# One table of numbers: the last quarter of the units in another order and in other PSUM banks

## What is computed

```python
def reference(x, txt, ...):
    # tok: patches -> tokens (einsum over 16x16 patches), layernorm, + positions, then
    x = ff(x); x = window_attention(x) + identity; x = ff(x) + x
    h = concatenate([x, txt], axis=1)                       # 96 tokens per sample
    # attn: h = h + L0_attn(layernorm(h)), which is
    x = x + ssm(ln(x))                                      # in_proj, conv of 4 taps, silu gates, out_proj
    x = x + attn(ln(x)) @ attn_proj_w + attn_proj_b         # 12 heads of 16
    x = x + gelu(ln(x) @ ffn1_w + ffn1_b) @ ffn2_w + ffn2_b # 192 -> 768 -> 192
    # ffn: h = h + L0_ffn(layernorm(h)), the gated stage, which is
    gates = top-2 of 10 routed experts' softmax, and 2 shared ones, one per head
    q, k, v = x @ qkv_w + qkv_b                             # 12 heads of 64
    q, k = layernorm(q), layernorm(k)                       # over the 64 of each head
    o = softmax(q * scale @ k.T) @ v
    return (gates * o) @ proj_w + proj_b
```

## Time and profile before

| | us |
|---|---|
| device time, median of 3 runs | 567.08 |
| the three runs | 565.38, 567.08, 567.1 |
| the profiled execution, its own time | 564.13 |
| its span, first to last instruction | 562.3 |
| TensorE busy | 515.8 (92%) |
| VectorE busy | 405.9 (72%) |
| ScalarE busy | 299.1 (53%) |
| GpSimd busy | 88.8 (16%) |

### The profile page before, as it was taken

The page is one execution under the profiler, slowest core; times in us unless marked ns, Lnnn a source line. Parts: engine busy times, 40 slices in busy tenths (PEclk is TensorE's granted clock), DMA queues, the critical chain, the costliest instruction groups (busy, mean ns, idle before and its releaser), DMA issues. The chain is left out here.

```text
span 562.3 us, 11393 instructions
## 1 busy us (share of the span) xinstructions
PE 515.8 (92%) x4691; PEld 395.9 (70%) x4691; DVE 405.9 (72%) x891; ACT 299.1 (53%) x489; POOL 88.8 (16%) x70
## 2 busy tenths in 40 slices
...
DMA packets 13443, 16.02 MB, mean 28 GB/s; under 512 B 6491, under 2 KB 10960, under 8 KB 13008
## 3 DMA queue, kind: packets, MB, share of 16 engines
...
## 5 line engine op out<-in xcount | busy, mean ns | idle before, releaser
L1733 DVE TENSOR_REDUCE smax<-ps 96x12 f32<-96x1152 f32 (+1 forms) x28 | 37.8, 1349 | 17.1 <-PE ps L1063 9.9
L1747 DVE TENSOR_REDUCE psum<-pr 128x12 f32<-128x1152 f32 (+1 forms) x24 | 32.3, 1345 | 5.0 <-ACT pr L1386 4.9
L1381 ACT ACTIVATE pr<-ps,less 128x96 f32<-128x96 f32 (+1 forms) x96 | 24.6, 337 | 18.3 <-DVE less L1735 18.2
L1424 ACT ACTIVATE squares<-ps 128x1536 f32<-128x1536 f32 x12 | 17.4, 1450 | 28.4 <-PE ps L705 20.9
L1846 DVE TENSOR_REDUCE ss<-squares 128x24 f32<-128x1536 f32 x12 | 21.0, 1749 | 13.5 <-ACT squares L1424 13.4
L1975 POOL TENSOR_TENSOR side_wide<-attn,w_mask 128x1024 f32<-128x1024 f32 (+1 forms) x12 | 20.7, 1748 | 59.1 <-ACT attn L1276 47.4
L2001 POOL TENSOR_TENSOR squares<-squares,qk_root 128x512 f32<-128x512 f32 x8 | 16.6, 2081 | 75.6 <-DVE qk_root L1516 75.6
L685 PE MATMUL ps<-w_cqkv,side_c 64*96 64x384 f32 (+1 forms) x96 | 27.4, 500 | 0.0
L1949 POOL TENSOR_TENSOR ln_root<-ln_root,minus_half 128x3 f32<-128x3 f32 x8 | 6.9, 856 | 127.3 <-DVE ln_root L1621 127.3
L695 PE MATMUL ps<-w_cqkv,side_c 128*128 128x512 f32 (+1 forms) x72 | 26.2, 510 | 0.0
L1012 PE MATMUL ps<-w_ff,b_kB 128*128 128x192 f32 x144 | 25.5, 329 | 0.0
...
## 6 DMA issues: line engine op xcount, KB each, us to landing
...
```

The source lines that it names most:

```text
L1381: m = act.activation(e[:, s % 2, h * N:(h + 1) * N], t[0:rows, h // 4, h % 4 * N:(h % 4 + 1) * N], ACT.Exp, scale=head ** -0.5, bias=less[ ...
L1424: act.activation(sq.rearrange("p (b n) -> p b n", b=3), t[:, :, :], ACT.Square).then_inc(w.S["sq"], 1)
L1733: dve.tensor_reduce(mx, t, AX.X, ALU.max).then_inc(w.S[stage + "_sub"], 1)
L1747: dve.tensor_reduce(psum[0:rows, s % 2, :], e, AX.X, ALU.add).then_inc(w.S[done], 1)
```

## The change

Only the numbers in `STEPS_TEXT` differ. The new table writes every index and bank out, so that each of its lines reads differently, but the first 323 units keep their place and their bank, up to and with `b_e.1:3` just behind the last group's values. Of the 89 units from there on most stand in another order or in other banks:

```diff
-    e_e.3:2 e_n.2:2 e_pr.0:2=0 e_pt.2:2=5 e_n.3:2 b_f2.2:3 e_o.2:2=6 e_pt.3:2=3 e_pr.1:2 e_o.3:2=3 e_pr.2:2=7 c_u:3=3
...
+    e_s.1:2=0 e_n.0:2 e_e.0:2 e_e.1:2 b_f2.0:3=7 e_qt.2:2=4 e_n.1:2 b_f2.1:3=0 b_f2.2:3=1 e_pt.0:2=2 e_s.2:2=5
+    e_o.0:2=3 e_pt.1:2=0 e_v.2:2=3 e_e.2:2 c_u.0:3=0 e_o.1:2=3 e_v.3:2=6 e_n.2:2 e_s.3:2=3 e_pt.2:2=0 e_pr.0:2=6
+    e_e.3:2 e_n.3:2 c_qk.0:3=0 c_qk.1:3=5 e_o.2:2=3 e_pt.3:2=0 e_pr.1:2=4 c_g.0:3=2 c_qt.0:3=5 e_o.3:2=3 c_qt.1:3=0
+    c_s.0:3=5 c_e.0:3 e_pr.2:2=4 c_n.0:3 c_qk.2:3=0 c_v.0:3=3 c_v.1:3=6 c_s.1:3=3 c_pt.0:3=0 c_e.1:3 c_qt.2:3=0
```

More of the change, by code:

```diff
@@ L70 @@
 STEPS_TEXT = """
[L71 to L100, removed]
@@ L101 @@
-    e_e.3:2 e_n.2:2 e_pr.0:2=0 e_pt.2:2=5 e_n.3:2 b_f2.2:3 e_o.2:2=6 e_pt.3:2=3 e_pr.1:2 e_o.3:2=3 e_pr.2:2=7 c_u:3=3
-    c_g:3 c_qk.0:3=4 c_qk.1:3 c_qk.2:3=5 c_v.0:3 c_qt.0:3=2 c_qt.1:3 c_s.0:3=0 c_e.0:3 c_s.1:3=5 c_n.0:3 c_e.1:3
-    c_n.1:3 c_qt.2:3 c_v.1:3=3 c_pt.0:3 c_s.2:3 c_o.0:3=6 c_n.2:3 c_e.2:3 c_v.2:3 c_pt.1:3 c_s.3:3=5 c_o.1:3 c_e.3:3
-    c_pt.2:3 c_pr.0:3=3 c_v.3:3=6 c_o.2:3=0 c_pt.3:3=3 c_n.3:3 c_pr.1:3=2 c_o.3:3 c_pr.2:3=1
+    warm.4:0=0 warm.5:0=1 warm.6:0=2 warm.7:0=3 d_en.0:0 d_em.0:0=7 warm.8:0=0 warm.9:0=1 warm.10:0=2 warm.11:0=3
@@ new lines @@
+    d_x0.0:0=6 warm.12:0=5 a_bc.0:0=4 d_f1.0:0=1 a_en.0:1 a_em.0:1=4 d_f2.0:0=5 d_h2.0:0=2 a_x0.0:1=4 d_qk.0:0=5
+    a_f1.0:1=2 d_v.0:0=6 d_e.0:0 d_s.0:0=0 a_f2.0:1=3 a_h2.0:1=6 d_pt.0:0=4 d_s.1:0=0 d_e.1:0 a_qk.0:1=2 d_o.0:0=7
+    d_pt.1:0=0 a_tb.0:0=5 d_ot.0:0=6 d_o.1:0=4 a_wc.0:0 warm.2:0=2 a_pb.0:0=3 d_ot.1:0=2 a_e.0:1 d_pr.0:0=0 a_s.0:1=6
+    a_wc.1:0 d_f1.1:0=3 a_e.1:1 a_s.1:1=0 d_f2.1:0=2 d_h2.1:0=6 warm.1:0=7 d_ht.0:0=3 a_pt.0:1=0 a_v.0:1=6 a_o.0:1=2
+    d_u.0:0=3 a_pt.1:1=0 a_wc.2:0 d_in.0:0=2 a_ot.0:1=7 a_o.1:1=1 a_ot.1:1=7 warm.0:0=3 d_cv.0:0 a_pr.0:1=5 d_in.1:0=0
```

28 lines of the change are left out of this document (added).

## The result

The changed kernel takes 558.47 us (median of 6 runs), the kernel before, run beside it, 566.23: ratio 0.9888, 95% interval 0.9862 to 0.9914. The profiled execution took 558.12 us, its span is 556.3 (564.13 and 562.3 before).

A forecast was written before the change was run, and what follows sets the result against it. Neither VectorE nor TensorE was full; two chains that could overlap waited in turn. 6.2 us in the stretch plus 0.2 ahead gave 6.4, so 560.7 us from the 567.08 median; own range 558.5 to 562.6, recorded range 557.6 to 564.2.

The forecast's parts named there:

- Two chains behind each other were the loss: Stage e of group 2 and stage c of group 3 run in sequence; VectorE and TensorE wait in turn, 12.8 us.
- The stretch shortens by 6.2, with 6.6 us of waits left: From stage e's first maximum block to the end of `c_n.2:3`: VectorE's waits go from 12.8 to 6.6 us.
- Ahead of the stretch 0.2 earlier: Before stage e's first maxima: attention's projection some 1.5 later, less TensorE work behind it, net 0.2 us earlier.
- the bound on the other side: Ahead of stage e's first maxima: 1.5 us later if VectorE paces what follows and nothing is won back.
- The clock's 1.7 are won: Granted clock of 0.50 at 504.90 to 508.20 cost some 1.7 us; counted as won, within the 12.8 of waits.
- The tail keeps its length: From 544.28 to the last add at 559.52, one chain of matmuls and evictions: 15.24 us, order unchanged.
- The sum of 6.4: Total gain: 6.2 us in the stretch plus 0.2 ahead of it; 557.7 profiled, 560.7 from the median.
- the recorded one: Range 557.6 to 564.2 us, covering the forecast, the clock and the collision, and some spread of the runs.
- The clock did not fall again: Rival: clock falls behind a new pause at `c_qk.0` or `e_pr.1`; price 1.7 us, 562.4, chance 0.13.
- the tokens were read 6 us before TensorE wanted them: Rival: last group's tokens come late at `c_qk.0` and both chains stand; up to 571.8 us, chance 0.04.
- no wait of VectorE there was over 1.01 us: Rival: new waits from banks and near ties at `c_qk.2`, `c_s.1`, `c_s.2` take 5 of 6.4; 565.8, chance 0.06.
- The collision: Rival: VectorE and GpSimd collide more in the new order; two stalls, 2.6 us, 563.3, chance 0.10.

The follow-up runs named there:

- back_sn: Changed kernel with the last group's `c_s.0` and `c_e.0` behind `e_pr.2` (stage e's last product) again; 0.9941 of the kernel before, stretch 73.64 us.
- back_gqtsn: Changed kernel with the gates, `c_qt.0`, `c_qt.1` and first sample's scores, exponentials and weights behind stage e's last product, two `c_qk` still forward; 1.0034 of before, stretch 77.58.
- back_all: Changed kernel with all moved stage c units behind stage e's last product again, third feed-forward tile and `c_u` still forward; 1.0149 of the kernel before.
- f2_cu: Kernel before with only the third feed-forward tile `b_f2.2` and `c_u` of group 3 moved forward; measured 1.0045 of the kernel before, stretch 78.71 us.
- before_warm: Kernel before, old order, with idle 128x256 products in TensorE's pauses around the gate product; 0.9986 of before, stretch 76.00 us, 1.64 less.

## Why the prediction was right, step by step

- *Two chains behind each other were the loss.* Right: `back_sn`, `back_gqtsn` and `back_all` take the interleaving away by steps and give 73.64, 77.58 and 85.93 against 71.69. The middle one, at a clock of 1.00 throughout, is the clean one. `f2_cu` comes from the other side: the old order with early tokens alone gives 78.71.
- *The stretch shortens by 6.2, with 6.6 us of waits left.* Measured 5.97. Predicted and measured: `e_n.2` 0.4 and 0.38; the add of `e_pr.0` 1.0 and 1.01; `e_n.3` 0.5 and 0.47; first root block 1.8 and 1.48; `c_n.0` 0.7 and 0.77; third root block 0 and 0; `c_n.1` 1.0 and 0.96; `c_s.2` 0.2 and 0; `c_n.2` 1.0 and 0.96. Together 6.0. The blocks themselves took 71.69 - 6.03 = 65.7, where I had summed 64.9: their lengths were measured between neighbours that overlap by 0.08, and each of the seven waits that are left takes one such overlap away, some 0.6 of the 0.8. The kernel before has the same error: its waits of this kind add up to 11.7 (5.3, 1.8, 1.7, 1.6, 1.0 and 0.3), not to 12.8. So it drops out of the difference almost whole.
- *Ahead of the stretch 0.2 earlier.* This is the step that failed: 0.59 later, from a term that is small beside the others. Up to VectorE's layernorm it was right: `e_v.0` 1.1 later against `b_qk.0:3` (1.0 said), `b_o` and `u` 1.7 later (1.5 said), and TensorE had that back by its first wide product of `e_qk.1` (448.41, 0.05 later). What followed was paced by VectorE, as in the bound on the other side: its root block started 1.35 later, ScalarE's squares waited for it, and TensorE for the squares. A row each, of VectorE, ScalarE and TensorE:

```profile
455.48 1.74 DVE L1850 TENSOR_REDUCE ss<-squares 128x24 f32<-128x1536 f32 x1
...
457.31 1.45 ACT L1428 ACTIVATE squares<-ps 128x1536 f32<-128x1536 f32 x1 [1.82 <-DVE ss L1850]
...
460.25 1.25 PE L709 MATMUL ps<-bT,w_ff 64*128 64x192 f32 x12 [0.41 <-ACT squares L1431]
```

  By the means of four traces each the changed front costs 0.5, and the delay of `e_v.0` alone 1.0: it reached the stretch whole, where I had it paid back. I had let a delay of TensorE be paid back by less work for TensorE, and not asked whether VectorE, which inherits the delay, has the slack too.
- *The clock's 1.7 are won.* Right: the stretch runs at 1.00, and `before_warm` prices the term alone at 1.64.
- *The tail keeps its length.* Right: 15.26 against 15.24.
- *The sum of 6.4.* The traces give 5.4 for what the change does (5.97 - 0.59), the ratio 566.23 x 0.0112 = 6.3, interval 4.9 to 7.8, and the two medians differ by 7.8. Against the profiled execution the forecast was 557.7 and 558.12 was measured, but that is nearer than the sum deserves: 0.66 of the 6.0 comes from the part ahead of `b_qk.0:3`, which the change does not touch, and is luck. Of the two terms, 0.2 was missing in the stretch and 0.8 ahead of it. The forecast of 560.7 is 2.2 above the measured median of 558.47, which lies 0.03 below the forecast's own range of 558.5 to 562.6, though inside the recorded one. Of the 2.2, 0.85 is the median it started from (567.08 of three runs, 566.23 of six), and 1.4 is what the medians differ by beyond the 6.4; no trace shows a cause for that, and the ratio's interval covers it.
- *Rivals.* The clock did not fall again in the stretch, the tokens were read 6 us before TensorE wanted them (ScalarE's read ended at 485.70, the first product of `c_qk.0` started at 491.62), and no wait of VectorE there was over 1.01 us but that of the first root block (1.48). The collision did not come twice: one small operation was slow, as before, and in stage e's gates; this time it was the multiplication behind the comparison:

```profile
449.64 1.44 DVE L1811 TENSOR_TENSOR gsm<-gsm,w_prio 96x40 f32<-96x40 f32 x1
...
449.63 1.40 POOL L1997 TENSOR_TENSOR hx<-hx,w_ff_b 128x576 f32<-128x576 f32 x1
```
